# Turning normalized tiles and query/key stacks in 32 by 32 squares on VectorE with transfers by way of DRAM, in the long rounds of a macaron transformer block

## The chip, the cores and the metric

One core of a Trainium2 chip runs the whole program. The metric is the device time of one execution in microseconds; lower is better.

## What is computed

A macaron block on x of shape 8 x 512 x 512 (batch, sequence, width), all in float32:

```
x = x + 0.5 * ffn(layernorm(x))
x = x + attention(layernorm(x))
x = x + 0.5 * ffn(layernorm(x))
ffn(x)  = (silu(x @ w_gate.T) * (x @ w_up.T)) @ w_down.T          # hidden width 2048
attention: q, k, v = split(x @ w_qkv); 16 heads of 32 columns
  q, k = unit_norm(q), unit_norm(k); rotary embedding on every other head
  softmax(causal(q k^T * q_gain)) v, then @ w_out
```

## The kernel before

Products keep float32's accuracy by splitting each operand into two f16 parts, high and low, and adding three f16 products (`three`, lines 1125 to 1129). The eight batches b go through one after the other. Two streams of work are woven together: the FFN stream, whose steps are pieces of `gate`, `up` and `down` (twelve matmuls of 256 columns, twelve more, and six of 512 columns), and the attention of one batch. The planner `order()` writes one list, ORDER, by hand-set weights: between two attention stages `fill(n)` puts as many FFN pieces as n "beats" come to, where the pieces left in the round are shared out over the beats left. The weights are in MANY (the long rounds b = 2 to 5) and FEW (rounds 0, 1, 6, 7). Each engine walks ORDER and runs its own part of every stage, in that order, so a wait on an engine holds up all its later stages.

A third kind of work goes into a side list, one entry per piece (`beside`): the layer norms. `normalize(after, b, u, tiles)` puts for each 128-token tile the stages stats, norm, turn and split at the piece offsets PACE = (0, 2, 3, 4), the second tile 3 later. u is 0, 1, 2 for the input of the first FFN, of attention and of the second FFN; t is the tile, 0 to 3. "norm" is VectorE's L949 into `xn`; "turn" is TensorE's four f32 transposes (L1150) into PSUM bank 3; "split" is ScalarE's copy to the high f16 part (L788) and VectorE's difference for the low part (L954). The side list is first in, first out. Where a stage must not run before a split, `until` puts further FFN pieces until it has come.

In a projection stage (`projections`) of a half hf of the heads, tile t goes through qkv (TensorE), squares and copies (ScalarE L795, L796, L800), unit norm (VectorE L992), rotation (GpSimd L708 to L713), then "stack": ScalarE casts queries and keys into `stk` (L809), VectorE adds the low parts (L998, L999). "stack turn" is eight f16 transposes on TensorE into PSUM banks 2 and 3 (L1241, L1245); "stack out" copies them with two ScalarE (L814) and two VectorE (L1004) copies into QT and KT; "stack high" has SP copy one third of the rows by two DMAs (L651, L653). `stk` is one buffer: the next tile's cast waits for the turn (`kt_ps`). After the fourth tile come fill("dup") and fill("turned"), then the first "scores max" (L1263), which waits for the copies of all four tiles. PSUM bank 3 is shared with other turns, and `bank3` places its users.

SP issues all DMAs in ORDER: stores, loads and "stack high".

Of the kernel before, what the change touches and what calls it, by code (L numbers as in the profile page):

```python
# [21 lines left out]
ACT = mybir.ActivationFunctionType  # L22
# [4 lines left out]
P = 128  # L27
# [8 lines left out]
GH = 4  # L36
# [12 lines left out]
def build(nc, x, w_qkv, w_out, q_gain, w_gate, w_up, w_down, rope, out):  # L49
# [34 lines left out]
    xn += [WQ.rearrange("p s k n -> p (s k n)").bitcast(F32)[:, i * D:(i + 1) * D] for i in range(2)]  # L84
    XT = [halves(n).rearrange("p (s k n) -> p s k n", s=2, k=KC) for n in ("xt", "xt2")]
# [9 lines left out]
    KT = halves("kt").rearrange("p (h n) -> p h n", h=HH)  # L95
    V = halves("v").rearrange("p (t h c) -> p t h c", t=TT, h=HH)
# [40 lines left out]
    identb = sb("identb", P, BF16)  # L137
# [63 lines left out]
    def w_stats(j, first=0, n=4):  # L201
# [7 lines left out]
    FUSED = range(B)  # L209
# [4 lines left out]
        x_in0 x_in1 stored0 stored1 x1_done x2_done out_ready var_ready rstd_ready xn_done xt_ps xt_hi xt_lo  # L214
        qk_ps v_ps qs_done sq_done vhi_done vlo_done ssq_ready r_ready qn_done rope_done
        st_hi st_lo qt_ps kt_ps qt_ev kt_ev qt_dup kt_dup s1_ps smax_done mst_done mt_ps mt_copied mrow_done
# [5 lines left out]

    PARK = nc.dram_tensor("park", (2, TH, D), F32, kind="Internal").ap()
# [36 lines left out]

    def order():
# [27 lines left out]
        def normalize(after, b, u, tiles):  # L289

            stage = {}
            for i, t in enumerate(tiles):
                for n, name in zip(PACE, ("stats", "norm", "turn", "split")):
                    stage.setdefault(3 * i + n, []).append((name, b, u, t))
            for n in range(max(stage) + 1):
                side.append((after, sorted(stage.get(n, []), key=lambda x: ("split", "turn", "norm", "stats").index(x[0]))))
# [61 lines left out]
        def projections(b, hf, w):  # L358
            for t in range(TT + 1):
# [155 lines left out]
        while at[0] < len(pieces):  # L515
# [20 lines left out]

    def xn_of(b, u, t):

        if (b, u) == (0, 0) and t < 2:
            return 2 + t  # L540
        return t % 2 if (b, u) in ((0, 0), (B - 1, 2)) else 0

    def tile_no(b, hf, t):
        return (2 * b + hf) * TT + t

# [30 lines left out]
    with nc.Block() as block:  # L576

        @block.sync
        def _(sp):
# [67 lines left out]
            def stack_high(b, hf, t):  # L647

                c = slice(t * P, (t + 1) * P)
                sp.wait_ge(s["qt_ev"], tile_no(b, hf, t) + 1)  # L650
                sp.dma_start(QT[2 * HD:ST, :, c], QT[0:HD, :, c]).then_inc(s["qt_dup"], 16)  # L651
                sp.wait_ge(s["kt_ev"], tile_no(b, hf, t) + 1)
                sp.dma_start(KT[2 * HD:ST, :, c], KT[HD:2 * HD, :, c]).then_inc(s["kt_dup"], 16)  # L653

            run({"store": store, "load": load, "stack high": stack_high})
# [4 lines left out]
        def _(pool):  # L660
# [7 lines left out]
            for m in (ident, ident16, identb, maskq):  # L668
                link(nc.gpsimd.memset(m[:, :], 0.0))
# [7 lines left out]
            for m in (ident, ident16, identb):  # L677
# [63 lines left out]
        def _(act):  # L741
# [31 lines left out]
            def split(b, u, t):  # L773
                act.wait_ge(s["xt_ps"], place_of_norm[b, u, t] + 1)
# [13 lines left out]
                nc.scalar.activation(xt_of(b, u, t)[:, 0], ps(3).rearrange("p (k n) -> p k n", k=KC), ACT.Copy).then_inc(s["xt_hi"], 1)  # L788
# [22 lines left out]
            def stack_out(b, hf, t):  # L811
                act.wait_ge(s["qt_ps"], tile_no(b, hf, t) + 1)
# [51 lines left out]
        def _(dve):  # L864
# [78 lines left out]
            def norm(b, u, t):  # L943
# [4 lines left out]
                xn_reader[i] = "xt_ps", k + 1  # L948
                V_.tensor_scalar(xn[i], x_of(b, u, t), mv[:, 2 * t:2 * t + 1], rstd[:, t:t + 1], ALU.subtract, ALU.mult).then_inc(s["xn_done"], 1)  # L949

            def split(b, u, t):
                dve.wait_ge(s["xt_hi"], place_of_norm[b, u, t] + 1)
                xt = xt_of(b, u, t)
                V_.tensor_tensor(xt[:, 1], ps(3).rearrange("p (k n) -> p k n", k=KC), xt[:, 0], ALU.subtract).then_inc(s["xt_lo"], 1)  # L954
# [40 lines left out]
            def stack(b, hf, t):  # L995
# [3 lines left out]
                V_.tensor_tensor(STK[:, :, 0:HD], q3[:, HH:2 * HH, :], STK[:, :, HD:2 * HD], ALU.subtract).then_inc(s["st_lo"], 1)  # L999

            def stack_out(b, hf, t):
                dve.wait_ge(s["kt_ps"], tile_no(b, hf, t) + 1)
# [7 lines left out]
            def row_max(b, hf, h, bank):  # L1010
                dve.wait_ge(s["s1_ps"], 3 * head_no(b, hf, h) + bank + 1)
                if b in FUSED:
                    V_.memset(carrier[:, bank:bank + 1], 0.0)
                for t in QBANKS[bank]:
                    w, col = (t + 1) * P, mnegv[:, t, h:h + 1]
                    ins = V_.tensor_tensor_reduce(out=ps(0, QSEG[t], w), in0=ps(0, QSEG[t], w), in1=maskq[:, S - w:S], scale=1.0, scalar=2 * MASKED,  # L1016
                                                  op0=ALU.add, op1=ALU.max, accum_out=col) if b in FUSED else V_.tensor_reduce(col, ps(0, QSEG[t], w), AX_X, ALU.max, negate=True)
                ins.then_inc(s["smax_done"], 1)

            def maxima(b, hf, g):  # L1020
# [5 lines left out]
                src, unit = mnegv[:, :, g * GH:(g + 1) * GH], -2.0 ** -12 if b in FUSED else 2.0 ** -12  # L1026
# [84 lines left out]
            def weights(n):  # L1111
# [5 lines left out]
                 "stats": stats, "norm": norm, "split": split, "gated": gated, "parts": parts, "residual": residual,  # L1117
# [4 lines left out]
        def _(pe):  # L1122
# [113 lines left out]
            def stack_turn(b, hf, t):  # L1236
                i = tile_no(b, hf, t)
                pe.wait_ge(s["st_lo"], i + 1)
                take(2, "qt_ev", i + 1)
# [3 lines left out]
                take(3, "kt_ev", i + 1)  # L1243
# [10 lines left out]
            def scores_max(b, hf, h):  # L1254
                if h == 0:
                    pe.wait_ge(s["qt_dup"], 16 * tile_no(b, hf, TT))
                    pe.wait_ge(s["kt_dup"], 16 * tile_no(b, hf, TT))
# [109 lines left out]
```

## Time and profile before

| what | value |
|---|---|
| median of 3 runs | 2738.82 us (2738.73 to 2738.93) |
| profiled execution, its own time | 2739.15 us |
| its span, first to last instruction | 2737.3 us |
| TensorE busy | 2689.7 us, 98% |
| VectorE busy | 1787.4 us, 65% |
| ScalarE busy | 1180.1 us, 43% |
| GpSimd busy | 528.4 us, 19% |
| granted TensorE clock | 0.999 |
| DMA moved | 47.71 MB, 17 GB/s |

Busy times are of one profiled execution on the core. TensorE's matmuls are pipelined, so the duration of one overlaps the next; the issue interval is read from the starts in the timeline.

### The profile page before, as it was taken

What the parts mean: (1) busy time and instruction counts of PE and PEld (TensorE: products, weight loads), DVE (VectorE), ACT (ScalarE), POOL (GpSimd) and SP (SyncE); (2) the same over time, 40 slices, a digit from 0 to 9 for tenths busy, and PEclk for the clock granted to TensorE, in tenths of its full rate; (3) what the DMA queues carried; (4) which work ended last, traced back from release to release, by engine and by line L of the source; (5) the groups of instructions that cost most, each with busy time, mean ns of one, the idle gap of its engine ahead of it and who ended that gap; (6) DMA issues with size and microseconds to landing.
All of it is one profiled execution on the core that took longest, in us unless ns stands there. A gap on an engine that the chain in (4) does not pass through costs nothing.

```text
span 2737.3 us, 55236 instructions
## 1 busy us (share of the span) xinstructions
PE 2689.7 (98%) x22208; PEld 1957.6 (72%) x22208; DVE 1787.4 (65%) x5152; ACT 1180.1 (43%) x2197; POOL 528.4 (19%) x820
## 2 busy tenths in 40 slices
PE   7999999999999999999999999999999999999999
PEld 6677766776777776777767777777777766776776
DVE  8866676667666665656656666675756766676643
ACT  6454544454344443444434444334343544353422
POOL 0012212222131302112030220302113131313100
PEclk9999999999999999999999999999999999999999
DMA  5100000000000000000000000000000000000000
GB/s 202 62 19 7 19 7 3 7 19 22 1 9 17 24 1 3 22 1 24 2 5 21 11 15 1 7 18 21 5 17 9 17 9 2 9 17 17 2 9 16
DMA packets 51407, 47.71 MB, mean 17 GB/s; under 512 B 36304, under 2 KB 36304, under 8 KB 50640
## 3 DMA queue, kind: packets, MB, share of 16 engines
q1 hardware_dynamic: 51152, 44.19, 5.1%
q8 instruction: 175, 2.87, 0.4%
q14 instruction: 80, 0.66, 0.1%
HBM read 26.35 MB, written 9.44 MB: 13 GB/s over the span
## 4 chain that ended last, share of the span: by engine, by line
PE 88%; DVE 7%; issue 2%; ACT 2%; POOL 0%; DMA 0%; DVEq 0%; ACTq 0%; POOLq 0%
PE psum L1127 26%; PE psum L1129 26%; PE psum L1128 26%; PE psum L1287 2%; PE psum L1263 2%; PE psum L1299 2%; PE psum L1150 1%; DVE arena L959 1%; DVE arena L961 1%; ACT arena L844 1%; PE psum L1300 1%; DVE arena L954 1%; PE psum L1245 1%; DVE ss L888 1%; DVE arena L1038 1%
## 5 line engine op out<-in xcount | busy, mean ns | idle before, releaser
L1127 PE MATMUL psum<-arena,WU 128*128 128x256 f16 x2048 | 558.3, 273 | 1.5 <-DVE WU L900 1.5
L1127 PE MATMUL psum<-arena,WG 128*128 128x256 f16 x2048 | 558.2, 273 | 1.5 <-DVE arena L954 1.5
L1129 PE MATMUL psum<-arena,WG 128*128 128x256 f16 x2048 | 558.1, 273 | 0.0
L1129 PE MATMUL psum<-arena,WU 128*128 128x256 f16 x2048 | 558.0, 272 | 0.0
L1128 PE MATMUL psum<-arena,WG 128*128 128x256 f16 x2048 | 558.0, 272 | 0.0
L1128 PE MATMUL psum<-arena,WU 128*128 128x256 f16 x2048 | 557.9, 272 | 0.0
L959 DVE SCALAR_TENSOR_TENSOR arena<-arena,psum 128x256 f32<-128x256 f32 x512 | 215.0, 420 | 424.8 <-ACT arena L844 422.2
L844 ACT ACTIVATE arena<-psum,tscale 128x256 f32<-128x256 f32 x512 | 242.1, 473 | 563.6 <-PE psum L1129 562.6
L1127 PE MATMUL psum<-WD,arena 128*128 128x512 f16 x1024 | 388.9, 380 | 5.9 <-DVE WD L1088 4.3
L1129 PE MATMUL psum<-WD,arena 128*128 128x512 f16 x1024 | 388.4, 379 | 0.0
L1128 PE MATMUL psum<-WD,arena 128*128 128x512 f16 x1024 | 388.4, 379 | 0.0
L720 POOL TENSOR_SCALAR_AFFINE_SELECT arena<-arena 128x128 f32<-128x128 f32 (+1 forms) x384 | 125.4, 341 | 1138.9 <-ACT arena L826 1138.7
L850 ACT ACTIVATE arena<-arena 128x256 f16<-128x256 f32 x512 | 212.5, 415 | 301.9 <-DVE arena L961 298.0
L826 ACT ACTIVATE arena<-psum,lnbias,hscale 128x512 f32<-128x512 f32 (+1 forms) x256 | 221.8, 882 | 150.7 <-PE psum L1287 145.8
L965 DVE TENSOR_TENSOR arena<-arena 128x256 f16<-128x256 f32 x512 | 219.6, 429 | 100.1 <-ACT arena L850 98.3
L1016 DVE CUSTOM_DVE_ANT_0 psum<-psum,maskq 128x512 f32<-128x512 f32 (+3 forms) x512 | 240.4, 512 | 12.2 <-issue 11.8
L695 POOL TENSOR_TENSOR rn<-ss,mhalf 128x16 f32<-128x16 f32 x64 | 193.3, 3020 | 269.2 <-DVE ss L979 268.9
L1127 PEld LDWEIGHTS psum<-arena,WG 128*128 128x128 f16 x2048 | 200.0, 98 | 52.3 <-issue 1.9
L1128 PEld LDWEIGHTS psum<-arena,WG 128*128 128x128 f16 x2048 | 200.3, 98 | 51.2
L961 DVE SCALAR_TENSOR_TENSOR arena<-arena,psum 128x256 f32<-128x256 f32 x512 | 215.3, 421 | 17.5
L1127 PEld LDWEIGHTS psum<-arena,WU 128*128 128x128 f16 x2048 | 200.0, 98 | 25.1 <-DVE WU L900 2.1
L1129 PEld LDWEIGHTS psum<-arena,WG 128*128 128x128 f16 x2048 | 200.1, 98 | 23.5
(147 smaller groups left out, 4359.3 us busy)
## 6 DMA issues: line engine op xcount, KB each, us to landing
arena<-in_L_attn_x SPq DMA_DIRECT2D x16, 512.0 KB, 3.7
arena<-arena SPq DMA_DIRECT2D x128, 64.0 KB, 2.1
out<-arena SPq DMA_DIRECT2D x16, 512.0 KB, 2.8
WD<-in_L_ffn_w_up SPq DMA_DIRECT2D x4, 1024.0 KB, 6.3
arena<-in_L_ffn_w_down SPq DMA_DIRECT2D x4, 1024.0 KB, 8.5
WD<-in_L_ffn_w_gate SPq DMA_DIRECT2D x3, 1024.0 KB, 7.1
arena<-in_L_attn_w_qkv SPq DMA_DIRECT2D x1, 3072.0 KB, 10.2
WD<-in_L_ffn_w_gate SPq DMA_DIRECT2D x2, 512.0 KB, 4.2
```

Of the source, the lines that this page charges most:

```text
L695: nc.gpsimd.tensor_tensor(rn[:, c], ss2[:, c], mhalf[:, :], ALU.pow).then_inc(s["r_ready"], 1)
L720: return nc.gpsimd.affine_select(out=blocks, in_=blocks, compare_op=ALU.is_ge, fill=0.0, base=0, pattern=[[0, n], [1, P]], channel_multipl ...
L826: nc.scalar.activation(P32[:, c], ps(0, 0, SW)[:, c], ACT.Exp, bias=lnbias[:, 0:1], scale=hscale[:, c1:c1 + 1]).then_inc(s["exp_done"], 1)
L844: nc.scalar.activation(fH[j % 2], ps(4 + j % 2, 0, TH), ACT.Tanh, scale=tscale[:, c:c + 1]).then_inc(s["tanh_done"], 1)
L850: nc.scalar.activation(H2(j)[0], fH[j % 2], ACT.Copy).then_inc(s["h_hi"], 1)
L959: V_.scalar_tensor_tensor(out=fH[j % 2], in0=fH[j % 2], scalar=1.0, in1=g, op0=ALU.add, op1=ALU.mult).then_inc(s["a_done"], 1)
L961: V_.scalar_tensor_tensor(out=fH[j % 2], in0=fH[j % 2], scalar=2.0 ** -50, in1=u, op0=ALU.mult, op1=ALU.mult).then_inc(s["gated"], 1)
L965: V_.tensor_tensor(H2(j)[1], fH[j % 2], H2(j)[0], ALU.subtract).then_inc(s["h_lo"], 1)
L1016: ins = V_.tensor_tensor_reduce(out=ps(0, QSEG[t], w), in0=ps(0, QSEG[t], w), in1=maskq[:, S - w:S], scale=1.0, scalar=2 * MASKED, op0=ALU ...
L1127: T_.matmul(o, lhs(0), rhs(0), start=first, stop=False)
L1128: T_.matmul(o, lhs(0), rhs(1), start=False, stop=False)
L1129: return T_.matmul(o, lhs(1), rhs(0), start=False, stop=last)
```

## The change

In the long rounds the transposes of TensorE give way to another path. For a token tile chosen by `by_dma(b, u, t)` the norm writes `xn` with its 32-column blocks reordered, VectorE transposes every 32 by 32 square in place ("blocks"), one DMA writes the tile to DRAM (TURN), four DMAs ("fetch") read it back so that each square stands in its rows, and ScalarE and VectorE split from SBUF instead of PSUM. The stages stand at SLOW = (0, 2, 3, 6, 10) pieces, the second tile APART = 9 later. For a stack in rounds BY_DMA = range(2, B - 2), that is 2 to 5, VectorE transposes the squares of `stk` in place after the low parts; SP writes them with four DMAs of 64-byte rows into DRAM (STACK) and then reads them with four DMAs into QT and KT, the third part included. ScalarE's cast of the next tile waits for the landing of the four writes (`st_out`), and the first scores wait for `st_in`. The weights MANY and one of FEW are new. An identity in bf16 and the branches on FUSED, which was true for every batch, are dropped.

```diff
+    BLOCKS = words("xn").rearrange("p (c k n) -> p k c n", c=4, k=KC)
+    TURNED = words("xn").rearrange("p (a n) -> p a n", a=4)
+    QK = arena[:, place["qt"][0]:place["qt"][0] + HH * S].bitcast(F16).rearrange("p (h n) -> p h n", n=S)
-    identb = sb("identb", P, BF16)
+    TURN = nc.dram_tensor("turn", (4, P // 4, 4, P), F32, kind="Internal").ap()
+    STACK = nc.dram_tensor("stack", (HD, 4 * HH, 4, HD), F16, kind="Internal").ap()
+    def by_dma(b, u, t):
+        return u == 0 and 3 <= b <= 6 or u == 1 and t < 2 and 3 <= b <= 6 or u == 2 and t >= 2 and 1 <= b <= 4
             for i, t in enumerate(tiles):
-                for n, name in zip(PACE, ("stats", "norm", "turn", "split")):
-                    stage.setdefault(3 * i + n, []).append((name, b, u, t))
+                dma = by_dma(b, u, t)
+                for n, name in zip(*((SLOW, ("stats", "norm", "blocks", "fetch", "split")) if dma else (PACE, ("stats", "norm", "turn", "split")))):
+                    stage.setdefault((APART if dma else 3) * i + n, []).append((name, b, u, t))
                     fill(w["stack"])
-                    bank3(("stack turn", b, hf, t - 1), ("stack out", b, hf, t - 1), ("stack high", b, hf, t - 1))
+                    if b in BY_DMA:
+                        put(("stack fetch", b, hf, t - 1))
+                    else:
+                        bank3(("stack turn", b, hf, t - 1), ("stack out", b, hf, t - 1), ("stack high", b, hf, t - 1))
-    MANY = {"qk": 1.32, "qk first": 1, "ends": 1.92, "stack": 2, "v first": 1.25, "turned": 1, "max first": 0.4,
+    BY_DMA = range(2, B - 2)
+    SLOW, APART = (0, 2, 3, 6, 10), 9
+    MANY = {"qk": 1.06, "qk first": 1, "ends": 3.6, "stack": 1.6, "v first": 1.25, "turned": 1, "max first": 0.48,
             "maxima": 1, "max rows": 1, "scores": 1, "exp": 1.5, "high": 1, "low": 1, "max": 1,
-            "head": 1, "end": 0.8, "end values": 0.5, "out 0": 2, "out 1": 2, "out 2": 1.5, "out 3": 1,
-            "dup": 3}
-    FEW = {"qk": 1, "qk first": 2, "ends": 2.4, "stack": 2, "v first": 2.25, "turned": 1, "max first": 0.32,
+            "head": 1, "end": 1.0, "end values": 0.5, "out 0": 1.6, "out 1": 2, "out 2": 1.5, "out 3": 1,
+            "dup": 8.0}
+    FEW = {"qk": 1.5, "qk first": 2, "ends": 2.4, "stack": 2, "v first": 2.25, "turned": 1, "max first": 0.32,
...
+            def stack_blocks(b, hf, t):
+                if b in BY_DMA:
+                    sp.wait_ge(s["st_turned"], fetch_no(b, hf, t) + 1)
+                    for a in range(4):
+                        sp.dma_start(STACK[:, :, a], stk[HD * a:HD * (a + 1), 0:2 * D].rearrange("i (k n) -> i k n", n=HD)).then_inc(s["st_out"], 16)
+            def stack_fetch(b, hf, t):
+                sp.wait_ge(s["st_out"], 64 * (fetch_no(b, hf, t) + 1))
+                c, of = slice(t * P, (t + 1) * P), STACK.rearrange("i k a n -> i k (a n)")
+                for part in range(2):
+                    sp.dma_start(QK[HD * part:HD * (part + 1), :, c], of[:, part::2]).then_inc(s["st_in"], 16)
+                sp.dma_start(QT[2 * HD:ST, :, c], of[:, 0:2 * HH:2]).then_inc(s["st_in"], 16)
+                sp.dma_start(KT[2 * HD:ST, :, c], of[:, 2 * HH + 1::2]).then_inc(s["st_in"], 16)
+            def blocks(b, u, t):
+                sp.wait_ge(s["xt_turned"], place_of_turn[b, u, t] + 1)
+                sp.dma_start(TURN.rearrange("a i c n -> (a i) (c n)"), words("xn")).then_inc(s["xt_out"], 16)
+            def fetch(b, u, t):
+                sp.wait_ge(s["xt_out"], 16 * (place_of_turn[b, u, t] + 1))
+                for c in range(4):
+                    sp.dma_start(TURNED[32 * c:32 * (c + 1)], TURN[:, :, c].rearrange("a i n -> i a n")).then_inc(s["xt_in"], 16)
...
             def stack(b, hf, t):                       # ScalarE
                 act.wait_ge(s["rope_done"], i + 1)
-                if t:
-                    act.wait_ge(s["kt_ps"], i)
+                if t and b in BY_DMA:
+                    act.wait_ge(s["st_out"], 64 * fetch_no(b, hf, t))
+                elif t:
+                    act.wait_ge(s["kt_ps"], turn_no(b, hf, t))
...
             def norm(b, u, t):                         # VectorE
-                V_.tensor_scalar(xn[i], x_of(b, u, t), mv[:, 2 * t:2 * t + 1], rstd[:, t:t + 1], ALU.subtract, ALU.mult).then_inc(s["xn_done"], 1)
+                if by_dma(b, u, t):
+                    to, of = BLOCKS, of.rearrange("p (k c n) -> p k c n", k=KC, c=4)
+                V_.tensor_scalar(to, of, mv[:, 2 * t:2 * t + 1], rstd[:, t:t + 1], ALU.subtract, ALU.mult).then_inc(s["xn_done"], 1)
+            def blocks(b, u, t):
+                dve.wait_ge(s["xn_done"], place_of_norm[b, u, t] + 1)
+                V_.transpose(xn[0], xn[0]).then_inc(s["xt_turned"], 1)
             def stack(b, hf, t):
+                if b in BY_DMA:
+                    dve.wait_ge(s["st_lo"], tile_no(b, hf, t) + 1)
+                    V_.transpose(stk[:, 0:2 * D], stk[:, 0:2 * D]).then_inc(s["st_turned"], 1)
...
             def scores_max(b, hf, h):                  # TensorE
                 if h == 0:
+                    if b in BY_DMA:
+                        pe.wait_ge(s["st_in"], 64 * fetch_no(b, hf, TT))
```

## Rows read from the trace of the kernel before

**Rows 1.** The page: the span, busy times by engine, shares of the last-ending chain.
```profile
span 2737.3 us, 55236 instructions
PE 2689.7 (98%) x22208; PEld 1957.6 (72%) x22208; DVE 1787.4 (65%) x5152; ACT 1180.1 (43%) x2197; POOL 528.4 (19%) x820
PE 88%; DVE 7%; issue 2%; ACT 2%; POOL 0%; DMA 0%; DVEq 0%; ACTq 0%; POOLq 0%
```

**Rows 2.** Windows (length, then busy per engine, clock): rounds 2 and 5, heads stage.
```profile
764.00:1049.00 285.00, 284.05 (x2397) 207.17 (x2396) 182.36 (x551) 123.96 (x228) 53.07 (x88) 1.00 0.04 12
1715.00:2047.00 332.00, 331.40 (x2753) 241.78 (x2751) 212.41 (x624) 138.64 (x260) 64.13 (x100) 1.00 0.04 12
1270.00:1366.00 96.00, 96.00 (x846) 71.45 (x845) 65.38 (x212) 44.18 (x78) 8.68 (x26) 1.00 0.01 2
```

**Rows 3.** Timeline of TensorE, round 3: start, duration, line, shape and count.
```profile
1245.67 0.39 PE L1241 MATMUL psum<-ident,arena 128*128 128x128 f16 x4
1246.12 0.38 PE L1127 MATMUL psum<-WQ,arena 128*128 128x512 f16 x1
...
1250.02 0.38 PE L1127 MATMUL psum<-WD,arena 128*128 128x512 f16 x1
...
1253.93 0.39 PE L1241 MATMUL psum<-ident,arena 128*128 128x128 f16 x4
...
1262.21 0.60 PE L1150 MATMUL psum<-ident,arena 128*128 128x128 f32 x4
1262.64 0.38 PE L1127 MATMUL psum<-WD,arena 128*128 128x512 f16 x1
...
1270.35 0.71 PE L1263 MATMUL psum<-arena 96*128 96x512 f16 x4
```

**Rows 4.** Groups of TensorE by form: busy time and mean ns of one.
```profile
L1150 PE MATMUL psum<-ident,arena 128*128 128x128 f32 x376 | 56.5, 273 | 1.2 <-DVE arena L949 1.1
L1245 PE MATMUL psum<-ident,arena 128*128 128x128 f16 x256 | 24.9, 220 | 2.2 <-DVE arena L954 1.0
L1241 PE MATMUL psum<-ident,arena 128*128 128x128 f16 x256 | 24.7, 219 | 0.0
```

**Rows 5.** Waits of TensorE's weight loads, 760 to 2047 us.
```profile
PEld psum L1245 <- DVE arena L954: 2.8, 7, 1.1
```

**Rows 6.** Groups of VectorE by form: busy time and mean ns of one.
```profile
L1004 DVE COPY arena<-psum 64x512 f16<-64x512 f16 x128 | 53.9, 421 | 43.3 <-PE psum L1245 42.4
L949 DVE TENSOR_SCALAR arena<-arena,mv,rstd 128x512 f32<-128x512 f32 x94 | 50.9, 541 | 8.0 <-POOL rstd L690 7.7
```

**Rows 7.** Timelines of ScalarE and VectorE in round 3.
```profile
1250.68 0.65 ACT L809 ACTIVATE arena<-arena 128x512 f16<-128x512 f32 x1
...
1258.87 0.62 ACT L809 ACTIVATE arena<-arena 128x512 f16<-128x512 f32 x1
...
1252.03 0.42 DVE L999 TENSOR_TENSOR arena<-arena 128x256 f16<-128x256 f32 x1
```

**Rows 8.** Timeline of SP's DMA issues, round 3.
```profile
1247.32 0.59 SPq L651 DMA_DIRECT2D arena<-arena  x1
1247.94 0.61 SPq L653 DMA_DIRECT2D arena<-arena  x1
```

**Rows 9.** DMA view, 1247 to 1251 us; issues on the page (KB, us to landing).
```profile
DMA packets 544, 0.13 MB, mean 33 GB/s; under 512 B 544, under 2 KB 544, under 8 KB 544
q1 hardware_dynamic: 544, 0.13, 15.4%
arena<-arena SPq DMA_DIRECT2D x2, 64.0 KB, 2.1
...
out<-arena SPq DMA_DIRECT2D x16, 512.0 KB, 2.8
...
park<-arena SPq DMA_DIRECT2D x2, 512.0 KB, 3.7
```

**Rows 10.** Timeline of the first microseconds.
```profile
9.83 3.65 PE L1159 MATMUL psum<-ident,WD 128*128 128x128 f32 x16 [9.83 <-ACT WD L746]
```

More of the change, by code:

```diff
@@ L208, in build @@
     PCOLS = (slice(0, 512), slice(512, SW))
-    FUSED = range(B)
     OUT_BANK = (2, 0, 1, 2)
@@ L292, in normalize @@
             for i, t in enumerate(tiles):
-                for n, name in zip(PACE, ("stats", "norm", "turn", "split")):
-                    stage.setdefault(3 * i + n, []).append((name, b, u, t))
+                dma = by_dma(b, u, t)
+                for n, name in zip(*((SLOW, ("stats", "norm", "blocks", "fetch", "split")) if dma else (PACE, ("stats", "norm", "turn", "split")))):
+                    stage.setdefault((APART if dma else 3) * i + n, []).append((name, b, u, t))
             for n in range(max(stage) + 1):
-                side.append((after, sorted(stage.get(n, []), key=lambda x: ("split", "turn", "norm", "stats").index(x[0]))))
+                side.append((after, sorted(stage.get(n, []), key=lambda x: ("split", "fetch", "turn", "blocks", "norm", "stats").index(x[0]))))
         def next_side():
@@ L535, in build @@
     place_of_norm = {norm: k for k, norm in enumerate(norms)}
+    turned_by = {False: [n for n in norms if not by_dma(*n)], True: [n for n in norms if by_dma(*n)]}
+    place_of_turn = {n: k for way in turned_by.values() for k, n in enumerate(way)}
     def xn_of(b, u, t):
@@ L540, in xn_of, with turn_no, fetch_no @@
             return 2 + t
-        return t % 2 if (b, u) in ((0, 0), (B - 1, 2)) else 0
+        return t % 2 if (b, u) in ((0, 0), (B - 1, 2)) and not by_dma(b, u, t) else 0
     def tile_no(b, hf, t):
         return (2 * b + hf) * TT + t
+    def turn_no(b, hf, t):
+        return tile_no(b, hf, t) - (2 * TT * len(BY_DMA) if b >= BY_DMA.stop else 0)
+    def fetch_no(b, hf, t):
+        return tile_no(b - BY_DMA.start, hf, t)
     def head_no(b, hf, h):
@@ L666, in link @@
                 pool.wait_ge(s["pool_pro"], n[0])
-            for m in (ident, ident16, identb, maskq):
+            for m in (ident, ident16, maskq):
                 link(nc.gpsimd.memset(m[:, :], 0.0))
@@ L676, in _ @@
             link(nc.gpsimd.memset(halves("v"), 1.0))
-            for m in (ident, ident16, identb):
+            for m in (ident, ident16):
                 link(nc.gpsimd.affine_select(out=m[:, :], in_=m[:, :], compare_op=ALU.not_equal, fill=1.0,
@@ L811, in stack_out @@
             def stack_out(b, hf, t):
-                act.wait_ge(s["qt_ps"], tile_no(b, hf, t) + 1)
+                act.wait_ge(s["qt_ps"], turn_no(b, hf, t) + 1)
                 for odd in range(2):
@@ L1238, in stack_turn @@
                 pe.wait_ge(s["st_lo"], i + 1)
-                take(2, "qt_ev", i + 1)
+                take(2, "qt_ev", turn_no(b, hf, t) + 1)
                 for m in range(HH // 2):
@@ L1242, in stack_turn @@
                 ins.then_inc(s["qt_ps"], 1)
-                take(3, "kt_ev", i + 1)
+                take(3, "kt_ev", turn_no(b, hf, t) + 1)
                 for m in range(HH // 2):
@@ L1262, in scores_max @@
                         w = (t + 1) * P
-                        ins = T_.matmul(ps(0, QSEG[t], w), QT[0:ST, h, t * P:(t + 1) * P], KT[0:ST, h, 0:w], start=True, stop=b in FUSED)
-                        if b not in FUSED:
-                            ins = T_.matmul(ps(0, QSEG[t] + t * P, P), identb[:, :], maskq[:, S - P:S], start=False, stop=True)
+                        ins = T_.matmul(ps(0, QSEG[t], w), QT[0:ST, h, t * P:(t + 1) * P], KT[0:ST, h, 0:w], start=True, stop=True)
                     ins.then_inc(s["s1_ps"], 1)
```

43 lines of the change are left out of this document (26 added, 17 removed).

## The prediction

> **What bounds the kernel now.** I read the page's busy line and chain first. TensorE is busy 2689.7 of 2737.3 us and holds 88% of the chain that ended last [rows 1]. Next came the time windows by round. In the four long rounds TensorE is idle for only 0.6 to 1.0 us of 285 to 334 us, at the full clock, while VectorE is busy about 64% and ScalarE 42%; in a stage of attention heads VectorE reaches 68% [rows 2]. So a TensorE instruction taken out of a long round is worth its full issue time, as long as nothing that TensorE waits for gets later; and the other engines have room. The profiled execution took 2739.15 us, 1.85 more than its span; the median of the runs is 0.33 less. I make the sum on 2739.15.
>
> **What is removed from TensorE.** An f32 turn of one normalized tile (four squares) runs from 1262.21 to 1262.64, when the next matmul starts: 0.435 us. The two stack turns of a tile (eight f16 squares) run from 1245.67 to 1246.12: 0.45 us [rows 3]. The "mean ns" of the grouped view, 273 and 219, is latency with overlap and must not be multiplied by the count [rows 4]. Of the 96 turned token tiles, by_dma names 16 for u=0, 8 for u=1 and 8 for u=2: 32 x 0.435 = 13.9 us. BY_DMA holds rounds 2 to 5 with 8 stacks each: 32 x 0.45 = 14.4 us. Together 28.3 us, all of it on the path. With the turns go the waits for PSUM banks 3 and 2: the largest in these rounds is 2.8 us over 7 times [rows 5]; I take 1.5 us of gain, bounds 0 and 2.8.
>
> **What is moved to VectorE and ScalarE.** For a stack VectorE loses two copies of 421 ns and gets one square-wise turn of 1024 f16 columns. No row shows that operation. Bounds: the two copies, 0.84 us, and two of the 541 ns operations on 512 f32, 1.1 us, up to 1.4 for dearer [rows 6]; I take 1.1, since one result per lane and step is what the f32 row shows. A token tile adds a turn of 512 f32, 0.54 us by the same row (bounds 0.4 and 1.1). That is 32 x (1.1 - 0.84) + 32 x 0.54 = 26 us more VectorE time over 1283 us, two points of share: hidden. ScalarE loses its two evictions per stack, 1.2 us. The SBUF-to-SBUF split instead of one from PSUM I set to zero. The Trainium skill (VectorE: DVE Perf Modes, The three transpose paths) puts a 128x128 bf16 turn at 311 ns on VectorE and advises TensorE for a full 128x128 turn. An estimate from that figure is 8 x 0.311 = 2.5 us for a stack, which would lengthen the chain below by 1.4 us; no row here shows the operation. The page's advice is for one turn by itself, and here TensorE is what is short.
>
> **The new round trip of a stack, the term that decides.** Order: ScalarE's cast (L809), VectorE's two subtractions (L998, L999), the new turn, SP's four DMAs to DRAM, and only when all four have landed may ScalarE write the next tile's stack (the wait moved from kt_ps to st_out: stk has one buffer). Queued behind that wait on ScalarE are the tanh and cast of the FFN (L844, L850), for which VectorE and then TensorE wait. L809 starts at 1250.68 and L999 ends at 1252.45: 1.77 us [rows 7]. Turn 1.1. SP starts within 0.15 us (an assumption, small beside the rest). Issues follow each other every 0.62 us, so the fourth begins 1.86 us after the first [rows 8]. Landing of one such DMA: the nearest rows are 2.1 us (256 rows of 256 B, SBUF to SBUF), 2.8 us (512 KB into DRAM) and 3.7 us (to park) [rows 9]. Each of the four has 1024 rows of 64 B, 64 per DMA engine. Low: packets below the issue interval, 1.77 + 0.84 + 0.15 + 1.86 + 2.1 = 6.7 us. Taken: 1.77 + 1.1 + 0.15 + 1.86 + 2.8 = 7.7 us, call it T. High: a 64 B packet costs as much as a 256 B one. That one is 15.4% x 16 x 4 us / 544 = 18 ns [rows 9]; 256 of them per engine are 4.6 us after about 1.1 us to the first packet, plus about 1 us of receipt: T = 1.77 + 1.1 + 0.15 + 1.1 + 4.6 + 1.0 = 9.7 us. I lean to the low half because a packet a quarter as long should cost less than 18 ns.
>
> **How much time it has.** A piece of FFN (12 matmuls of 256 columns or 6 of 512) takes (1253.93 - 1250.02) / 3 = 1.30 us and a qkv 1246.12 to 1250.02, 3.90 us [rows 3]. In the planner's order a long round has 192 pieces. Of round 3's, 171 are left when tile 2 of the first half is projected, for 175.5 beats of MANY: 0.974 piece per beat. After the change two things lower this. The slow path of u=2 tiles 2 and 3 (9 + 10 + 1 = 20 stages) stands in the one side list ahead of u=1 tiles 2 and 3, so the `until` of qkv tile 2 pulls some 12 more pieces ahead: 159 are left. The new weights sum to 186.2 beats: 0.854. Moving pieces costs TensorE nothing by itself. From one stack to the next lie one qkv and (1.06 + 1.6) x 0.854 pieces, 3.90 + 2.95 = 6.85 us; the last gap, (1.6 + 1.06 + 3.6) x 0.854 pieces, is 6.95. The excess of T over 6.85 adds up from tile to tile (three gaps in the second half; two in the first, where the long `until` resets it). From the last stack to the first scores lie (1.6 + 8 + 1) x 0.854 = 9.05 pieces, 11.8 us, and ScalarE runs about 1 us ahead of its place in the order (before: 7 pieces and three turns, 10.4 us by count, 11.5 us from L809 at 1258.87 to L1263 at 1270.35 [rows 3, 7]): 12.8 us. Needed: T, then SP's four reads, 0.15 + 1.86 + 2.3 = 4.3 us (2.3 assumed a little above the 2.1 row). With T = 7.7 the second half is late by 3 x 0.85 + 12.0 - 12.8 = 1.75 us, the first by 0.9; four rounds: 10.6 us. The FFN's own slack on ScalarE (its chain of tanh, two products, cast, difference takes some 2.2 us of at least 3.9) absorbs lags of about 1.7 us, and those gaps partly round up to whole pieces; I take 7 us.
>
> **Token tiles.** Turn, DMA out, four DMAs in: 0.54 + 0.15 + 2.8 + 0.15 + 1.86 + 2.3 = 7.8 us, against 7 pieces (9.1 us) or more from "blocks" to "split". Covered. Behind them on SP stand the stack's transfers and the stores and loads; in the second half of each long round two token tiles of the next batch meet the last stacks, and a late split holds ScalarE up: 0 taken, up to 4 rounds x 2 tiles x 1 us = 8 us for the range. **Prologue.** TensorE's first matmul waits for ScalarE's L746 until 9.83 us [rows 10], not for GpSimd's identities; dropping identb costs and brings nothing.
>
> **Sum:** 2739.15 - 28.3 - 1.5 + 7 = 2716.3 on the profiled execution, 2716 as a median.
>
> **Rivals.** (1) Everything is covered, T below 7.2: 2739.15 - 29.8 - 0.33 = 2709 us. For it: the low bound of T; against: a write to DRAM lands later than one to SBUF in every row. (2) Slower: the round trip through DRAM takes the place of TensorE as the bound. With T = 9.7 each gap loses 2.85 us: the second half 8.55 + 14.0 - 12.8 = 9.75 us, the first 6.9, four rounds 66.6 us: 2775 us. It decides from T = 8.4, where the loss of 2 x (T + 4.3 - 12.8) + 5 x (T - 6.85) is 7.4 us in a round and the gain is gone. For it: no row shows 64 B written to DRAM, and nothing in the issue row shows that 1024 rows are issued as fast as 256. The Trainium skill (DMA: Bandwidth & Descriptors, Specifications) says that below 512 B the DMA engine reads, modifies and writes, so is not at line rate; that rule would push T past the 18 ns case. The trace has 256 B rows at 18 ns each, 14 GB/s per engine, written to SBUF, and none in DRAM. (3) No change, T between 8.2 and 8.6: about 2739. (4) The change does not do what it says, TensorE's freed time being idle because pieces come no faster: it would need VectorE or ScalarE near 100%, and rows 2 speak against it; it falls together with (3).
>
> **Chances.** Forecast case (2712 to 2733) 0.45; rival (1) 0.27; (3) and (4) together 0.08; rival (2) 0.20. A measurement of this kernel tells about 0.2% (5.5 us) from no change: faster 0.72, same 0.08, slower 0.20. The range has to hold the forecast, most of rival (1) (with 2.8 us instead of 1.5 it gives 2707.7) and the milder part of rival (2): 2707 to 2765.
>
> **What would show it.** The groups L1150, L1241 and L1245 shrink by 128 each (stacks) and by 128 (tokens); TensorE's idle time in windows of the long rounds stays under 2 us each if (1), some 2 us if the forecast, over 10 us if (2). The steps show in: the time from ScalarE's L809-like cast to the landing of the fourth DMA (7.7), a ScalarE wait for a DMA at the next stack (0.8 us, some 20 times), and a TensorE wait for a DMA at the first scores (0 to 2 us, 8 times). I am wrong if a 64 B row costs over 14 ns, or if one issue takes much over 0.62 us.

## The result, and the profile after

| kernel | us, median | against before |
|---|---|---|
| before | 2738.88 (2738.73 to 2739.54) | |
| after | 2764.86 (2763.58 to 2765.69) | 1.0094 (95%: 1.0082 to 1.0106) |

The change costs 26.0 us; the prediction had 2716 us, a gain of 23. The page of after, to be read against [rows 1]:

```profile
span 2764.0 us, 54685 instructions
...
PE 2676.4 (97%) x21824; PEld 1928.9 (70%) x21824; DVE 1820.5 (66%) x5152; ACT 1142.9 (41%) x2133; POOL 528.9 (19%) x818
...
PE 77%; DVE 10%; issue 4%; DMA 3%; SPq 3%; ACT 3%; POOL 0%; DVEq 0%; ACTq 0%; POOLq 0%
...
turn<-arena SPq DMA_DIRECT2D x32, 256.0 KB, 2.0
arena<-turn SPq DMA_DIRECT2D x128, 64.0 KB, 2.0
stack<-arena SPq DMA_DIRECT2D x128, 64.0 KB, 2.7
arena<-stack SPq DMA_DIRECT2D x64, 128.0 KB, 2.9
```

The first reading is what did not fail: 384 instructions have left TensorE (22208 to 21824) and its busy time fell by 13 us. The span grew all the same, so TensorE stands idle elsewhere. Its share of the chain fell from 88% to 77%; VectorE, the DMAs and SP's queue, which held 7, 0 and 0%, hold 10, 3 and 3%. The idle time stands in the long rounds. Windows of after (length, then busy per engine with instructions, granted clock, DMA share, GB/s), of which the second is the stretch of the second row of [rows 2], where TensorE was idle for 0.6 us:

```profile
1424.00:1756.00 332.00, 323.20 (x2625) 231.70 (x2624) 218.06 (x617) 128.54 (x241) 64.57 (x99) 0.99 0.15 35
1715.00:2047.00 332.00, 321.43 (x2606) 230.23 (x2604) 217.22 (x616) 126.04 (x239) 64.25 (x97) 1.00 0.16 36
```

Now it is 9 to 11 us in each, and VectorE and ScalarE are at 66 and 39%: nothing is full, something waits. The waits of after (engine and line waited at, what released it, us in total, times, longest):

```profile
ACT arena L864 <- DMA stack<-arena: 33.8, 18, 3.6
...
PEld psum L1334 <- DVE mneg L1084: 24.8, 47, 2.6
PE psum L1195 <- DVE arena L1031: 24.2, 13, 3.8
...
ACT arena L838 <- DMA arena<-turn: 22.4, 8, 6.2
...
PE psum L1334 <- DVE mneg L1084: 11.4, 13, 2.1
...
PE psum L1334 <- DMA arena<-stack: 3.3, 3, 2.6
```

L864 is ScalarE's cast of the next stack, L838 its split of a token tile, L1195 an FFN matmul, L1334 `scores_max` (L1263 before), L1084 the row maxima. ScalarE waits for transfers 56 us, TensorE directly for only 3.3: what TensorE sees of the round trips is the FFN's `down`, which gets its operand late (24.2 us, L1031 being the last link of tanh, product, cast, difference). A third thing has nothing to do with a transfer: score matmuls wait for row maxima.

One knot of it, the chain of after in round 3 (start, duration, what). L1068 is the square-wise turn, L683 the four writes of a stack, L690 to L692 its four reads, L696 and L702 a token tile's write and its four reads:

```profile
1260.56 1.25 DVE arena L1068
1261.83 0.58 SPq L683
1262.45 0.67 SPq L683
1263.16 0.67 SPq L683
1263.88 2.72 DMA stack<-arena
1266.67 0.64 ACT arena L864
...
1271.45 4.18 DMA stack<-arena
...
1275.65 0.57 SPq L690
1276.26 0.63 SPq L690
1276.93 0.62 SPq L691
1277.59 0.45 SPq L692
1278.09 0.45 SPq L696
1278.58 0.58 SPq L683
```

Two loops are closed here. ScalarE's: cast, differences, turn, four writes, landing, and only then the next cast. SP's: four writes, wait for the landing, four reads, and only then the next four writes, with a token tile's transfers in between. What the engines do meanwhile, ScalarE's timeline and then TensorE's (start, duration, line, shape; in brackets the idle time before it and its releaser):

```profile
1275.72 0.63 ACT L864 ACTIVATE arena<-arena 128x512 f16<-128x512 f32 x1 [3.63 <-DMA stack<-arena]
1276.25 0.46 ACT L899 ACTIVATE arena<-psum,tscale 128x256 f32<-128x256 f32 x1
...
1289.72 0.63 ACT L838 ACTIVATE arena<-arena 128x512 f16<-128x512 f32 x1 [3.13 <-DMA arena<-turn]
```

```profile
1276.62 0.27 PE L1197 MATMUL psum<-arena,WU 128*128 128x256 f16 x1
1280.37 0.61 PE L1195 MATMUL psum<-WD,arena 128*128 128x512 f16 x1 [3.48 <-DVE arena L1031]
```

ScalarE stands 3.63 us before the next stack; the tanh (L899) queued behind it starts when the stack has been cast; its `down` starts on TensorE after 3.48 us of nothing.

For comparisons finer than the windows I took every TensorE instruction's start, subtracted the issue time of its form, and added up what is left; this "lost time" is 54.0 us in before (1.3 to 2.6 in a long round) and 109.1 in after (20.7, 13.8, 12.6, 12.9 in rounds 2 to 5). The two numbers and the 28.3 us removed belong together by the way they are made: + 55.1 lost - 28.3 removed = + 26.8, which is the difference of the two spans (26.7). So this sum is no test of the 28.3; it says how much TensorE lost by waiting, and where.

### The profile page after: what moved, and what is told of

The parts are those of the page before. It is cut to its first block, busy times and chain, and to the rows that moved or that the text cites. A ratio compares the mean times of both kernels' runs of the same rounds, so it can differ in the third digit from the quotient of the medians.

```text
span 2764.0 us, 54685 instructions
## 1 busy us (share of the span) xinstructions
PE 2676.4 (97%) x21824; PEld 1928.9 (70%) x21824; DVE 1820.5 (66%) x5152; ACT 1142.9 (41%) x2133; POOL 528.9 (19%) x818
## 4 chain that ended last, share of the span: by engine, by line
PE 77%; DVE 10%; issue 4%; DMA 3%; SPq 3%; ACT 3%; POOL 0%; DVEq 0%; ACTq 0%; POOLq 0%
PE psum L1195 23%; PE psum L1197 23%; PE psum L1196 23%; PE psum L1356 2%; DMA stack<-arena 2%; PE psum L1334 2%; PE psum L1368 2%; SPq L683 1%; DVE arena L1025 1%; DVE arena L1068 1%; DVE arena L1027 1%; PE psum L1218 1%; PE psum L1369 1%; ACT arena L899 1%; DVE mneg L1084 1%
## 5 line engine op out<-in xcount | busy, mean ns | idle before, releaser
L1195 PE MATMUL psum<-arena,WG 128*128 128x256 f16 x2048 | 559.6, 273 | 1.5 <-DVE arena L1020 1.5
L1195 PE MATMUL psum<-arena,WU 128*128 128x256 f16 x2048 | 558.4, 273 | 1.5 <-DVE WU L955 1.5
L899 ACT ACTIVATE arena<-psum,tscale 128x256 f32<-128x256 f32 x512 | 241.6, 472 | 564.3 <-PE psum L1197 563.5
L1195 PE MATMUL psum<-WD,arena 128*128 128x512 f16 x1024 | 391.7, 383 | 28.6 <-DVE arena L1031 24.2
L1031 DVE TENSOR_TENSOR arena<-arena 128x256 f16<-128x256 f32 x512 | 219.2, 428 | 106.3 <-ACT arena L905 104.8
L1084 DVE CUSTOM_DVE_ANT_0 psum<-psum,maskq 128x512 f32<-128x512 f32 (+3 forms) x512 | 240.3, 511 | 23.9 <-issue 23.9
L1195 PEld LDWEIGHTS psum<-arena,WG 128*128 128x128 f16 x2048 | 200.6, 98 | 54.7 <-issue 3.3
L1195 PEld LDWEIGHTS psum<-arena,WU 128*128 128x128 f16 x2048 | 200.1, 98 | 25.1 <-DVE WU L955 2.1
```

The source lines that it names most:

```text
L899: nc.scalar.activation(fH[j % 2], ps(4 + j % 2, 0, TH), ACT.Tanh, scale=tscale[:, c:c + 1]).then_inc(s["tanh_done"], 1)
L1031: V_.tensor_tensor(H2(j)[1], fH[j % 2], H2(j)[0], ALU.subtract).then_inc(s["h_lo"], 1)
L1195: T_.matmul(o, lhs(0), rhs(0), start=first, stop=False)
```

## The experiments

Unless said otherwise the edits are against after, and every kernel computes the whole block. The kernel before took 2738.96 to 2739.31 us beside them.

**One part at a time.** The first four runs split the change into token tiles, stacks and weights.

`weights_only`: both detours off, the new weights kept.

```diff
-        return u == 0 and 3 <= b <= 6 or u == 1 and t < 2 and 3 <= b <= 6 or u == 2 and t >= 2 and 1 <= b <= 4
+        return False
-    BY_DMA = range(2, B - 2)
+    BY_DMA = range(2, 2)
```

> The new weights and stage lists with both transfers by DRAM switched off: every turn is back on TensorE. Theory A (the idle time comes from ScalarE waiting for transfers in the second projection stage): 2738 to 2743 us, TensorE idle in the long rounds as before, under 3 us a round. Rival W (the new weights starve the heads, so that TensorE waits for VectorE's row maxima): 2750 us or more, and the waits of the first scores for mneg stay at the 36 us of the changed kernel.

Measured: 2758.56 us, 1.0070 (1.0055 to 1.0085), that is 19.3 slower than before: rival W, and its sign too (the score matmuls and their weight loads wait for row maxima 36.7 us over the whole run, in before 18.9). The theory that pieces can be moved about for nothing is dead: moving them, with no transfer and no change of instructions, costs three quarters of the whole loss. A window and two waits of TensorE, 720 to 2060 us, where in before the wait of the weight loads was 3.8 us (20 times) and that of the matmuls did not show:

```profile
1715.00:2047.00 332.00, 328.38 (x2709) 237.73 (x2708) 209.57 (x616) 136.54 (x255) 63.34 (x97) 1.00 0.04 11
```

```profile
PEld psum L1334 <- DVE mneg L1084: 16.9, 33, 1.0
...
PE psum L1334 <- DVE mneg L1084: 5.3, 12, 0.5
PE psum L1368 <- DVE arena L1020: 4.7, 7, 1.2
```

Idle time in the window went from 0.6 to 3.6 us at full clock. The rows show two kinds of wait. The score matmuls (L1334) wait for row maxima. And the value matmuls of a head (L1368, into PSUM bank 3) wait for the difference (L1020) of a token tile whose turn stands in the same bank: with the pieces moved, turns and value products meet.

`tokens_only`: the token tiles' detour and the new weights.

```diff
-    BY_DMA = range(2, B - 2)
+    BY_DMA = range(2, 2)
```

> Only the token tiles go by DRAM; the stacks are turned on TensorE, with the new weights. 32 x 0.435 = 13.9 us less TensorE work. Theory A: the token trip alone is covered, 2724 to 2728 us. Rival T (the token trip itself is late, seen as 22 us of ScalarE waits for turn in the changed kernel): 2735 to 2745 us, with those waits still there.

Measured: 2737.13 us, 0.9991 (0.9981 to 1.0). Against weights_only that is 21.4 less, more than the 13.9 us of turns taken out: lost time falls too, from 73.3 to 66.1 us. The value matmuls' wait for L1020 (4.7 us in weights_only) is not among the waits of tokens_only: its token tiles are not in bank 3. The time is in the range of rival T, but T's sign did not come: ScalarE waits for a token tile once, 0.3 us. So the 22.4 us of that wait in after appear only where stacks stand on SP as well.

`stacks_only`: the stacks' detour and the new weights.

```diff
-        return u == 0 and 3 <= b <= 6 or u == 1 and t < 2 and 3 <= b <= 6 or u == 2 and t >= 2 and 1 <= b <= 4
+        return False
```

> Only the stacks go by DRAM; token tiles are turned on TensorE, with the new weights. 14.4 us less TensorE work. Theory A (stack loop of 7.8 us against gaps of 6.9 us, made worse by token transfers in the same SP queue): about half of the 54 us of new idle time stays, 2745 to 2755 us. Rival T (without the token transfers on SP the stacks are covered): 2725 to 2730 us.

Measured: 2764.48 us, 1.0091 (1.0076 to 1.0106), slower than both theories had it. Against weights_only, with the same pieces in the same places, the stacks' detour costs 5.9: it saves 14.4 and loses 20. No token tile is on SP here, and ScalarE still waits 23.7 us (12 times) for the landing of the last stack.

The parts add up to 2739.3 + 19.3 - 21.4 + 5.9 = 2743.1; together they take 2764.9. Some 22 us come only where both detours run. Their order differs as well: the token tiles' stages pull pieces ahead (`until`), so that in the second halves of rounds 3 to 5 the stacks and the first scores of after are 2, 2, 5 and 8 pieces apart, where in stacks_only they are 3, 2, 6 and 10 apart.

`tokens_old_weights`: the token tiles' detour with the weights of before.

```diff
-    BY_DMA = range(2, B - 2)
+    BY_DMA = range(2, 2)
-    MANY = {"qk": 1.06, ... "ends": 3.6, "stack": 1.6, ... "dup": 8.0}
+    MANY = {"qk": 1.32, ... "ends": 1.92, "stack": 2, ... "dup": 3}
-    FEW = {"qk": 1.5, ...
+    FEW = {"qk": 1, ...
```

> Only the token tiles go by DRAM, with the weights of the kernel before. Theory A: 2722 to 2728 us, the best of the four. If the weights matter for themselves it differs from the run with the new weights by more than 3 us.

Measured: 2738.32 us, 0.9996 (0.9987 to 1.0005). The expected 2722 to 2728 us did not come, and the difference from the run with the new weights is only 1.2 us, less than the 3 named. The 13.9 us are saved and 13.1 lost again (lost time 67.1 us). The detour of the u=2 tiles has 20 stages in the one side list, and `until` then pulls pieces forward: in ORDER the two halves of a round's heads have 53 and 48 pieces beside them instead of 57 and 53. That is a part of the mechanism of weights_only by another door; how large a part, tokens_few_old_weights tells.

**Which pieces matter.** `cover_only` is the kernel before with one number changed: the cover that after has between the last stack and the first scores.

```diff
-            "dup": 3}
+            "dup": 8.0}
```

> The kernel before with one weight changed, dup 3 -> 8 in the long rounds: 3 to 4 more pieces between the last stack and the first scores, as many fewer elsewhere. My prediction put the moving of pieces at 0: 2739 us. Theory W (pieces missing beside the row maxima and the other short stages leave TensorE waiting for VectorE): 2743 to 2752 us, TensorE's waits for mneg and mst above those of before.

Measured: 2750.69 us, 1.0042 (1.0029 to 1.0054); theory W. A window and the waits of TensorE, 720 to 2060 us:

```profile
1715.00:2047.00 332.00, 329.32 (x2730) 239.31 (x2729) 211.73 (x624) 138.50 (x259) 64.31 (x100) 1.00 0.04 11
```

```profile
PEld psum L1263 <- DVE mneg L1016: 15.1, 30, 1.0
```

```profile
PE psum L1263 <- DVE mneg L1016: 5.2, 14, 0.5
```

There is no detour in this kernel. A round has 192 pieces; what `dup` takes is missing beside the heads, where VectorE's row maxima hold the bank that the next scores need, and TensorE waits there 30 times up to 1.0 us. So one weight alone costs 11.6 us; all the new weights together cost 19.3.

`tokens_few_old_weights`: as tokens_old_weights, without the u=2 tiles.

```diff
-        return u == 0 and 3 <= b <= 6 or u == 1 and t < 2 and 3 <= b <= 6 or u == 2 and t >= 2 and 1 <= b <= 4
+        return u == 0 and 3 <= b <= 6 or u == 1 and t < 2 and 3 <= b <= 6
```

> Tokens by DRAM for u=0 and u=1 only (24 tiles), stacks on TensorE, weights of the kernel before. Without the 20-stage slow path of u=2 no pieces are pulled ahead of tile 2 of the first half (57 and 53 pieces in the heads, as before, against 53 and 48). Theory P (pieces missing in the heads are what ate 13 of the 13.9 us in tokens_old_weights): 24 x 0.435 = 10.4 us less, 2729 to 2731 us. Rival V (VectorE's added turns delay the row maxima): 2736 us or more.

Measured: 2734.70 us, 0.9984 (0.9976 to 0.9993). With 57 and 53 pieces beside the heads again, eight turns fewer saved (3.5 us) bring 3.6 us more. Of 24 x 0.435 = 10.4 us, 4.3 arrive; that is between the two theories. The 6.1 us that are still lost hardly come from missing pieces. From 720 to 2060 us the score matmuls wait 5.1 us (9 times) for row maxima, which in before does not show: there VectorE has the token tiles' work between its row maxima. tokens_few_later, below, is the test.

**The collision.** `tokens_later` is after with the token tiles that meet the last stacks started 12 pieces later.

```diff
-                        normalize(at[0] + LOAD, after[0], after[1], (2 * after[2], 2 * after[2] + 1))
+                        late_by = 12 if after[1] == 0 and after[2] == 1 and 3 <= after[0] <= 6 else 0
+                        normalize(at[0] + LOAD + late_by, after[0], after[1], (2 * after[2], 2 * after[2] + 1))
```

> The changed kernel, with one thing moved: the norms of tiles 2 and 3 of the first FFN's input (batches 3 to 6) start 12 pieces later, so that their transfers no longer stand among the stacks of the second half on SP. Work and every other stage are the same. Theory Q (token and stack transfers hold each other up in SP's one queue, and ScalarE waits for both; the two parts together cost some 22 us more than each alone): 2744 to 2750 us, the ScalarE waits for turn (22 us) nearly gone. Rival S (the stack loop of 7.8 us alone fills the gaps): at least 2760 us.

Measured: 2753.61 us, 1.0057 (1.0042 to 1.0073): 11.3 better than after, about half of the 22, and between the two theories. The waits for transfers:

```profile
ACT arena L865 <- DMA stack<-arena: 32.7, 18, 3.6
...
PE psum L1335 <- DMA arena<-stack: 5.1, 4, 2.3
...
ACT arena L839 <- DMA arena<-turn: 0.6, 1, 0.6
```

ScalarE's wait for token tiles is gone (22.4 to 0.6 us); its wait for the stacks stays at 33, so that one is not made by the token tiles. The stacks and the first scores stand at the same pieces as in after. On SP the meeting shows directly: in after the writes of the last stack of rounds 3 to 5 start 1.6 us after its turn has ended, in tokens_later 0.03 us.

`tokens_later_wide`: the same, with more pieces between two stacks.

```diff
-    MANY = {"qk": 1.06, ...
+    MANY = {"qk": 2.6, ...
```

> As tokens_later, and the weight qk of the long rounds 1.06 -> 2.6: three pieces instead of two between two stacks (7.8 us instead of 6.5), as long as the stack's loop. Theory Q: ScalarE's waits for the stack's writes (34 us in the changed kernel) fall under 10 us; 2738 to 2745 us. Rival W (pieces taken from the heads cost TensorE more at the row maxima): not faster than tokens_later.

Measured: 2769.79 us, 1.0113 (1.0099 to 1.0127): 16.2 slower than tokens_later, which is rival W. The wider gap does what it should, ScalarE's wait for the stacks falls from 32.7 to 4.4 us (L865). But the same rows show the price:

```profile
PEld psum L1335 <- DVE mneg L1085: 30.8, 68, 2.1
...
PE psum L1335 <- DVE mneg L1085: 12.1, 17, 1.8
PE psum L1335 <- DMA arena<-stack: 11.7, 5, 2.9
...
ACT arena L865 <- DMA stack<-arena: 4.4, 5, 2.7
```

The score matmuls wait for the row maxima 12.1 us instead of 7.0 and the weight loads 30.8 instead of 21.4; and everything after the stacks starts later too (token tiles 17.5 us again).

`all_trips_old_weights`: after with the weights of before, so the least cover.

```diff
-    MANY = {"qk": 1.06, ... "ends": 3.6, "stack": 1.6, ... "dup": 8.0}
+    MANY = {"qk": 1.32, ... "ends": 1.92, "stack": 2, ... "dup": 3}
-    FEW = {"qk": 1.5, ...
+    FEW = {"qk": 1, ...
```

> The changed kernel with the weights of the kernel before: gaps between stacks of 3 pieces (7.8 us and more), but only 6 pieces between the last stack and the first scores, 8 us against the 12 us that the trip takes. Theory: ScalarE waits little, TensorE waits 8 times some 4 us at the first scores, 2745 to 2760 us. If the weights' own cost (19 us in weights_only) weighs more, it is faster than the changed kernel by 10 us or more.

Measured: 2787.32 us, 1.0176 (1.0163 to 1.019), far above what was expected. Here the first scores stand openly before the reads of the stack, once in each of the 8 halves of the long rounds:

```profile
PE psum L1334 <- DMA arena<-stack: 33.5, 8, 6.2
```

So the cover is needed if the stacks go by DRAM, although it costs time by itself (11.6 us in the kernel before): with the stacks' detour in, the new weights are the smaller of two losses (2764.9 against 2787.3).

`two_stk_later`: tokens_later with a second buffer for the odd tiles' stacks, so that ScalarE waits for the tile before the last.

```diff
+    stk_odd = [at_word(place["yt"][0]), at_word(place["xn"][0])]
...
+    def stk_of(b, hf, t):
+        return stk_odd[hf] if t % 2 and 2 <= b < B - 2 else stk
...
                 if t and b in BY_DMA:
-                    act.wait_ge(s["st_out"], 64 * fetch_no(b, hf, t))
+                    if t > 1:
+                        act.wait_ge(s["st_out"], 64 * (fetch_no(b, hf, t) - 1))
```

> tokens_later with a second buffer for the odd tiles' stacks (in words that are free then), so that ScalarE waits for the landing of the stack before the last one, not of the last. Same order, same transfers. Theory L (ScalarE's wait for the stack's writes, 33 us in 18 waits in tokens_later, is what makes TensorE wait for L1032's difference, 10 to 13 us in the middle rounds): those waits vanish and the time falls by 8 to 15 us, to 2739 to 2746 us. Rival Q2 (SP's own loop, 4 writes, wait, 4 reads, some 7.2 us against 6.5 us of gap, keeps the trip late): ScalarE's waits vanish but TensorE waits for the reads at the first scores instead, under 4 us gained.

Measured: 2755.51 us, 1.0061 (1.0047 to 1.0075): no better than tokens_later (2753.6). Its waits:

```profile
PE psum L1350 <- DMA arena<-stack: 14.9, 6, 4.3
...
DVE arena L1022 <- DMA stack<-arena: 13.3, 4, 7.5
...
PE psum L1211 <- DVE arena L1046: 7.9, 3, 6.3
...
ACT arena L877 <- DMA stack<-arena: 1.3, 5, 0.4
```

ScalarE's wait is gone (32.7 to 1.3 us) and TensorE's for `down` is 7.9 instead of 17.9; its wait for the reads before the first scores rose from 5.1 to 14.9. These are the signs of rival Q2: the buffer was not the only bound. With ScalarE free, the loop on SP comes next: four issues of writes 2.0 us, landing 2.7, four issues of reads 2.5, so 7.2 us for a tile, in a gap of 6.5. In round 3 the writes of the four stacks of the second half start at 1261.49, 1268.73, 1276.02 and 1283.30, 7.3 us apart, while the casts come every 6.6 to 6.8 us; the last turn is over 1.8 us before its writes can start. The VectorE row is a cost of this edit's own: half of the second buffers stand in the words of `xn`, so the norm of one token tile waits for the last stack's writes. What a second buffer is worth without that cost was not run.

**What is left of use.** `tokens_few_later`: tokens_few_old_weights with the 12 pieces of tokens_later.

```diff
-        return u == 0 and 3 <= b <= 6 or u == 1 and t < 2 and 3 <= b <= 6 or u == 2 and t >= 2 and 1 <= b <= 4
+        return u == 0 and 3 <= b <= 6 or u == 1 and t < 2 and 3 <= b <= 6
...
-                        normalize(at[0] + LOAD, after[0], after[1], (2 * after[2], 2 * after[2] + 1))
+                        normalize(at[0] + LOAD + late_by, after[0], after[1], (2 * after[2], 2 * after[2] + 1))
```

> tokens_few_old_weights with the norms of tiles 2 and 3 of u=0 12 pieces later, behind the first row maxima of the second half. Theory V (there VectorE's norm, square turn and difference of two tokens run between the row maxima and hold them up; 1.7 us a round at L1334): 6 to 7 us faster, 2728 to 2730 us. Rival: the gaps move to the next group of maxima, 2733 to 2736 us.

Measured: 2730.21 us, 0.9968 (0.9956 to 0.998). This is faster than both kernels: 8.9 us less than the kernel before beside it, of the 10.4 us that its 24 turns are worth. Against tokens_few_old_weights it is 4.5 us, where theory V had 6 to 7; the cause is V's, since pieces and turns are the same and the wait for row maxima falls from 5.1 to 1.1 us. A window of it:

```profile
1715.00:2047.00 332.00, 331.30 (x2746) 240.76 (x2745) 218.31 (x635) 139.25 (x262) 64.72 (x101) 1.00 0.08 23
```

TensorE is idle for 0.7 us of the 332, nearly as in before. No wait of its matmuls for a transfer is left in the long rounds, and those for row maxima (L1335) are 1.1 us in all, 4 times.

## Why the prediction was wrong, point by point

**What is removed: right.** 384 instructions left. The best test is tokens_few_later: 24 turns taken out, almost no wait added, 8.9 of 10.4 us gained. "A TensorE instruction taken out is worth its full issue time, as long as nothing that TensorE waits for gets later" held as well; the condition is what broke. The 1.5 us from bank waits can't be told apart in these totals; with the new weights such waits are larger (4.7 us at L1368 in weights_only, none in tokens_only).

**The operation on VectorE: right.** The group of after, by form:

```profile
L1068 DVE STREAM_TRANSPOSE arena<-arena 128x1024 f16<-128x1024 f16 x32 | 39.8, 1245 | 1.1
```

1.245 us against 1.1 taken (0.84 to 1.4). The 2.5 us that were estimated from the 311 ns of the Trainium skill (VectorE: DVE Perf Modes, The three transpose paths) are twice too high here: the row gives 156 ns for 128 columns when one instruction turns 1024.

**The round trip T: right in size.** From the cast's start to the turn's it is 1.46 us in most of the 32 stacks (1.77 taken), the turn is 1.25, and in the chain above the writes run from 1261.83 to the last landing at 1266.60, 4.8 us: 7.5 us, where 7.7 was taken. The parts came out otherwise, the issues slower (0.67 for 0.62) and the turn longer, the rest shorter. Other stacks take longer (the row of 4.18 us): read in this way from the trace, the time from cast to last landing is 7.5 to 9.2 us over the 32 stacks, with a median of 7.9. The price of a packet, on which rival (2) hung, is in the DMA view of after from 1260 to 1268 us, where 4096 of the packets are those of four writes:

```profile
DMA packets 4166, 0.26 MB, mean 33 GB/s; under 512 B 4166, under 2 KB 4166, under 8 KB 4166
q1 hardware_dynamic: 4166, 0.26, 27.4%
```

27.4% x 16 x 8 us / 4166 = 8.4 ns for a packet of 64 B, half of the 18 ns of one of 256 B [rows 9], and below the 14 ns named as the mark. So the mechanism of rival (2) as it was priced did not come, although its figure, 2775 us, was the nearest. The measured 2764.9 is also just inside the stated range, whose upper end was set for that rival; that is luck. The rule of the Trainium skill (DMA: Bandwidth & Descriptors, Specifications) that below 512 B the engine reads, modifies and writes so that it is not at line rate, agrees with the trace as far as the rate goes: 64 B in 8.4 ns are 7.6 GB/s an engine, where 256 B in 18 ns were 14. Whether the engine reads first is not shown, and no stack of after reached the 9.7 us that the rule was to push T beyond.

**How much time it has: mis-sized.** The beats were worked out as averages; ORDER holds whole pieces. In the second half of a long round the stacks stand at pieces 876, 878, 880 and 885 and the first scores at 893: gaps of two pieces and a qkv or of five pieces, 6.5 us for 6.85 and 6.95, and 8 pieces of cover for 9.05 (10 in the first half). The sum put ScalarE's lag at 0.85 us a gap "some 20 times"; 7.9 against 6.5 us makes 1.4, and measured are 18 waits, 33.8 us in all, 1.9 us each. What else stands on SP (1.6 us at the last stack) was put at 0, and SP's own loop was not set against the gap: it takes 7.2 us, longer than the gap too, and bounds as soon as ScalarE does not (two_stk_later). "The FFN's own slack absorbs lags of about 1.7 us" held for the small ones, and the larger show as 3.5 us gaps of `down`. Taken were 7 us; stacks_only lost 20 against weights_only.

**Token tiles, 0 taken, up to 8: too low.** The bound of 8 us came from 1 us for each of 8 meetings with the last stacks. The eight meetings took place, with 22.4 us of ScalarE's time, and undoing them brought 11.3 us on TensorE. Nothing was charged for what the token tiles do away from SP: pieces that `until` pulls away from later stages, and VectorE's work between the row maxima. With the old weights the two cost 13.1 us (tokens_old_weights).

**"Moving pieces costs TensorE nothing by itself": the step that failed.** It was one sentence, with no row behind it, and it is worth 19.3 us (weights_only); `dup` alone costs 11.6 (cover_only). What the runs showed in its place: TensorE then waits for row maxima and for PSUM bank 3. The row of the heads stage was read in part: VectorE is at 68% on average there and TensorE at 96.00 of 96 us [rows 2], which says that the pieces were enough where they stood, not that any can be spared. The number of pieces beside the heads is not the whole of it: by ORDER tokens_only has fewer of them than weights_only and lost less.

**The sum put right.** 2739.15 - 28.3 + 19.3 (weights) + 20.3 (stacks' loop: 5.9 + 14.4) = 2750.5; tokens_only lost 7.5 us less than its turns explain, which makes it 2743, and the two detours together bring 22 more. The waits for bank 3, which go with the turns (4.7 us), account for most of the 7.5 by their size. Of the 22, 11.3 are the meeting on SP and ScalarE. What stands behind the other 11 stays open. Two things differ that no run took apart: the shorter gaps of after (2, 2, 5 and 8 pieces for 3, 2, 6 and 10), and its longer time at the lower clock (20.4 us for 6.8 in stacks_only, see the last section).

**What was said would show it.** "Over 10 us idle in a window if (2)" is about what the windows show (8.8 and 10.6 us). "A TensorE wait for a DMA at the first scores, 0 to 2 us, 8 times": 3.3 us in all, 3 times, right. The case that was given 0.20 came by its signs, but its cause was put in the packet, while the runs show it in the order of the pieces and in what stands on SP.

## What to carry to other kernels

Where one engine is full and the order of its work has been tuned, the work that lies between short stages of another engine is itself a resource: an edit that shifts it must be priced by running it with nothing else changed (here 19.3 us), and time saved on the full engine arrives only if that work stays where it was. Price a transfer that an in-order queue issues as a loop (issue, wait for landing, read back) against the interval between two of them, and list who else stands in that queue at that moment. Take such a detour where its queue is free and its users are late (the 24 token tiles of tokens_few_later), and leave it where the result is wanted within few microseconds.

## What the runs showed of the hardware

After an idle stretch TensorE's granted clock can fall to its lower level, 1.2 GHz, which no long round of before shows. Windows of after, the third of which follows the 3.48 us of idle time shown above:

```profile
942.40:945.80 3.40, 3.23 (x10) 1.41 (x11) 3.26 (x10) 0.42 (x1) 2.33 (x4) 0.51 0.73 109
962.80:969.60 6.80, 5.13 (x18) 1.98 (x17) 5.68 (x27) 1.83 (x4) 0.00 (x0) 0.50 0.00 0
1280.30:1283.70 3.40, 3.33 (x10) 1.50 (x11) 1.19 (x4) 0.42 (x1) 2.21 (x4) 0.50 0.59 67
```

With two more at 795.6 and 1628.4 this is 20.4 us at half speed in the long rounds, so up to 10 us of the lost time (the engine waited in part of it anyway). Between 720 and 2080 us such stretches come in the kernels whose matmuls wait 2 us and more there (6.8 us of them in stacks_only, 10.2 in tokens_later, and some in tokens_later_wide, all_trips_old_weights and two_stk_later), and in none of weights_only, cover_only or the kernels with the token tiles' detour alone, where no matmul waits over 1.5 us for another engine. No run took the clock away by itself, so its share is not settled. An idle TensorE can cost more than its idle time here, and that was no term of the prediction.
